# Four-layer graph network: the residual of the node stages formed per tile from PSUM, two small layer-norm operations on ScalarE

## What is computed

```
x = layernorm(x + L0(x, ...))      # out = self(x) * attr + conv * attr^2 ...
x = layernorm(x + L1(x, ...))
x = layernorm(x + L2(x, ...))
x = layernorm(x + L3(x, ...))      # cos(angle) * scfeat + sin(angle) * conv
layernorm(x) = (x - mean(x)) / sqrt(var(x) + 1e-5)
```

## Time and profile before

| | us |
|---|---|
| median of 3 runs | 4850.13 (4847.89 to 4857.97) |
| the profiled execution, its own time | 4907.07 |
| its span (first to last instruction) | 4905.3 |
| mean granted TensorE clock in it | 0.871 of full |
| busy in the span: PE / DVE / ACT / POOL | 3837.4 / 3538.7 / 2331.3 / 3500.2 |
| node stage of layer 0, first to last L1344 | 785.4 to 1222.0 |
| node stage of layer 1 | 2507.4 to 2761.6 |
| node stage of layer 2 | 3461.0 to 3741.7 |
| node stage of layer 3 | 4422.0 to 4897.8 |

### The profile page before, as it was taken

One profiled execution on the slowest core, in us unless ns is written; L12 is line 12 of the kernel. 1 busy time (PEld: TensorE's weight loads), 2 busy tenths in 40 slices (PEclk: granted clock), 3 DMA queues, 4 the chain that ended last, 5 costly groups with the idle time before them and its releaser, 6 DMA issues. The chain is left out here.

```text
span 4905.3 us, 72936 instructions
## 1 busy us (share of the span) xinstructions
PE 3837.4 (78%) x14102; PEld 1906.9 (39%) x14102; DVE 3538.7 (72%) x8505; ACT 2331.3 (48%) x6704; POOL 3500.2 (71%) x3640
## 2 busy tenths in 40 slices
PE   1999996776699999999920288888897888877666
PEld 0333334554244444444310133333674333335554
DVE  1666667999488888888868554544896555549999
ACT  0233323555455555555446543433896333335555
POOL 1666667999578877887634466666697666659998
PEclk9999997877799999999955598998998999988777
DMA  9222225665455555545469622222995222237665
GB/s 392 67 67 67 69 67 176 213 214 189 106 125 129 130 126 129 123 124 124 108 227 368 222 67 65 67 65 58 323 355 187 67 68 67 68 86 211 192 189 160
DMA packets 585571, 718.23 MB, mean 146 GB/s; under 512 B 79012, under 2 KB 409194, under 8 KB 585224
## 3 DMA queue, kind: packets, MB, share of 16 engines
q1 hardware_dynamic: 492812, 536.17, 36.1%
q0 software_dynamic: 86400, 142.71, 11.2%
q10 hardware_dynamic: 6268, 38.40, 1.9%
HBM read 488.77 MB, written 245.93 MB: 150 GB/s over the span
## 5 line engine op out<-in xcount | busy, mean ns | idle before, releaser
L539 POOL DMA_INDIRECT aggregates<-agg_out,scatter_index x600 | 615.8, 1026 | 400.9 <-issue 258.0
L1285 ACT ACTIVATE y_chunk<-residual,ln_minus_mean_rstd,ln_rstd 128x160 f32<-128x160 f32 x1568 | 691.7, 525 | 372.9 <-POOL ln_minus_mean_rstd L1348 287.9
L1344 POOL TENSOR_TENSOR ln_rstd<-ln_var_eps,minus_half 128x4 f32<-128x4 f32 x392 | 485.1, 1238 | 143.3 <-DVE ln_var_eps L1433 84.4
L1251 PE MATMUL psum<-self_weights,x_chunk_T 128*128 128x160 f32 (+1 forms) x2352 | 493.0, 362 | 64.7 <-DVE node_mid L1376 31.0
L522 POOL DMA_INDIRECT gathered<-x_layer,gather_index x400 | 395.5, 989 | 177.2 <-issue 118.6
L1251 PEld LDWEIGHTS psum<-self_weights,x_chunk_T 128*128 128x128 f32 x2352 | 414.1, 224 | 110.4 <-issue 63.2
L615 PE MATMUL psum<-identity,scaled_x 128*128 128x128 f32 x600 | 145.8, 282 | 373.6 <-DVE scaled_x L689 312.4
L1441 DVE BATCH_NORM_STATS2 ln_stats<-residual 128x6 f32<-128x160 f32 x1568 | 389.2, 307 | 0.1
L561 ACT ACTIVATE scaled_x<-gathered,sh_times_attr 128x160 f32<-128x160 f32 x400 | 138.4, 417 | 459.7 <-DVE sh_times_attr L672 307.0
L1329 POOL TENSOR_TENSOR agg_chunk<-agg_chunk,x_chunk 128x640 f32<-128x640 f32 x196 | 327.5, 1671 | 15.4
L638 PE MATMUL psum<-hidden,weights 64*128 64x512 f32 x300 | 185.8, 702 | 193.4 <-ACT hidden L573 131.4
(11 more groups left out here) (222 smaller groups left out, 10592.5 us busy)
## 6 DMA issues: line engine op xcount, KB each, us to landing
x_layer<-y_chunk SPq DMA_DIRECT2D x294, 320.0 KB, 5.3
x_chunk<-x_layer SPq DMA_DIRECT2D x294, 320.0 KB, 4.7
agg_chunk<-aggregates SPq DMA_DIRECT2D x196, 320.0 KB, 5.5
sh_rows<-in_sh_big SPq DMA_DIRECT2D x50, 768.0 KB
agg_chunk<-aggregates SPq DMA_DIRECT2D x98, 384.0 KB, 6.0
aggregates<-zero_rows ACTq DMA_DIRECT2D x1, 36864.0 KB
x_chunk<-in_x SPq DMA_DIRECT2D x98, 322.0 KB, 3.0
agg_chunk<-aggregates SPq DMA_DIRECT2D x98, 322.0 KB, 3.7
```

Source lines behind the costliest of these rows:

```text
L539: eng.indirect_dma_start(agg_table[:, :], bass.IndirectOffsetOnAxis(idx_last[:, q, b:b + 1], 0), agg_out[:, q, b, :], None, bounds_check=N ...
L1251: eng.matmul(o[:, b, 0:ns + 96], x_t[:, k4, (2 * half + b) * 128:(2 * half + b) * 128 + 128], self_w[:, k, 0:ns + 96], start=b == 0, stop= ...
L1285: op = eng.activation(y_out[:, buf, b, :], res[:, buf, b, :], ACT.Identity, bias=shift[:, buf, b:b + 1], scale=rstd[:, buf, b:b + 1])
L1344: eng.tensor_tensor(rstd[:, buf, :], var_eps[:, q, :], minus_half[:, 0:T], ALU.pow)\
```

## The change

In layers 0 and 3 the multiplication out of PSUM (L1376) and the addition (L1395) become one operation per tile, four per chunk, that reads PSUM, multiplies by a per-partition scalar and adds `agg_in`, and writes `res` directly. It stands where the multiplication stood in the step. It waits for what both waited for (`u_mm`, in layer 3 `half`, `agg_x`, and `applied` of four chunks before), and PE's wait for the PSUM buffer and POOL's for its buffer are now on `res`. In all four layers the two small operations on mean and variance leave DVE and stand on ACT, after L1285 and ahead of L1292, with the same waits. A constant column with epsilon is set up for them. Everything else stays.

```diff
@@ node_tensor
-                    wait(eng, S["mid"] if l == 2 else S["u_scaled"], c - 1)
+                    wait(eng, S["mid"] if l == 2 else S["res"], c - 1)
@@ node_scalar, after the four operations of L1285
+                lag = SUM[l] + 1
+                if live(s, lag, NC):
+                    c, buf, q = s - lag, (par - lag) % RB, (par - lag) % 2
+                    eng.wait_ge(S["aggr"], at(S["aggr"], c + 1))
+                    wait(eng, S["rstd"], c - 1)
+                    wait(eng, S["shift"], c - 1)
+                    eng.activation(var_eps[:, q, :].unsqueeze(2), mv[:, buf, :, 1:2], ACT.Identity, bias=eps_col[:, 0:1])\
+                       .then_inc(S["eps"], 1)
+                    eng.activation(neg_mean[:, q, :].unsqueeze(2), mv[:, buf, :, 0:1], ACT.Copy, scale=-1.0)\
+                       .then_inc(S["neg_mean"], 1)
@@ node_gpsimd
-                        wait(eng, S["u_scaled"], c - 1)
+                        wait(eng, S["res"], c - 1)
@@ node_vector, scaled_u
+                wait(eng, S["applied"], c - 3)
                 if l == 3:
                     eng.wait_ge(S["half"], at(S["half"], c + 1))
-                    by = turned[:, q, 0, :]
-                else:
-                    by = attr_all[:, bass.ds(c * T, T)]
-                eng.tensor_tensor(mid[:, q, :, 0:D], u[:, :, 0:D], by.unsqueeze(2).to_broadcast([128, T, D]), ALU.mult)\
-                   .then_inc(S["u_scaled"], 1)
+                eng.wait_ge(S["agg_x"], at(S["agg_x"], c + 1))
+                for b in range(T):
+                    by = turned[:, q, 0, b:b + 1] if l == 3 else attr_all[:, bass.ds(c * T + b, 1)]
+                    op = eng.scalar_tensor_tensor(out=res[:, r, b, :], in0=u[:, b, 0:D], scalar=by,
+                                                  in1=agg_in[:, buf, b, 0:D], op0=ALU.mult, op1=ALU.add)
+                op.then_inc(S["res"], 1)
@@ node_vector, residual
-                eng.wait_ge(S["u_scaled"], at(S["u_scaled"], c + 1))
-                eng.wait_ge(S["agg_x"], at(S["agg_x"], c + 1))
-                eng.tensor_tensor(res[:, r], mid[:, q, :, 0:D], agg_in[:, buf, :, 0:D], ALU.add).then_inc(S["res"], 1)
@@ node_vector, step: gone
-                    eng.tensor_scalar(var_eps[:, q, :].unsqueeze(2), mv[:, buf, :, 1:2], EPS, None, ALU.add)\
-                       .then_inc(S["eps"], 1)
-                    eng.tensor_scalar(neg_mean[:, q, :].unsqueeze(2), mv[:, buf, :, 0:1], -1.0, None, ALU.mult)\
-                       .then_inc(S["neg_mean"], 1)
```

More of the change, by code:

```diff
@@ L139, in gnn_kernel @@
         ones_col = sb("ones_column", [128, 1])
+        eps_col = sb("epsilon_column", [128, 1])
         ones_row = sb("ones_row", [1, GE])
@@ L258, in gnn_kernel @@
                                  "neg_mean res rstd shift stats store0 store1 store2 store3 tail transposed trig turn u_mm "
-                                 "u_scaled xt_copied")
+                                 "xt_copied")
         NODE = {l: node_sems for l in range(4)}
@@ L287, in node_counts @@
             if l not in (0, 3):
-                n.update(agg_scaled=0, agg_x=0, u_scaled=0)
+                n.update(agg_scaled=0, agg_x=0)
             n.update(turn=4 * NC, trig=NC, half=NC) if l == 3 else n.update(turn=0, trig=0, half=0)
@@ L318, in apart @@
         def apart(eng):
-            eng.wait_ge(P["consts"], 3)
+            eng.wait_ge(P["consts"], 4)
         def apart_from(eng, value):
@@ L391, in setup_gpsimd @@
             eng.memset(ones_col[:, :], 1.0).then_inc(P["consts"], 1)
+            eng.memset(eps_col[:, :], EPS).then_inc(P["consts"], 1)
             eng.memset(ident[:, :], 0.0).then_inc(P["ident0"], 1)
@@ L1263, in node_scalar @@
             S = NODE[l]
+            if l == 0:
+                eng.wait_ge(P["consts"], 4)
             def step(s, par):
@@ L1310, in step @@
                     held(eng, loaded(l, c, buf), S[f"load{buf}"])
-                    held(eng, c - 1, S["u_scaled"])
+                    held(eng, c - 1, S["res"])
                     held(eng, c * T)
@@ L1360, in node_vector, with scaled_u @@
             S = NODE[l]
-            def scaled_u(c, buf, q):
+            def scaled_u(c, buf, q, r):
                 u = psum[:, 4 + 2 * q:6 + 2 * q, :].rearrange("p a (b c) -> p (a b) c", c=256)
@@ L1405, in step @@
                 if l != 1 and live(s, U[l], NC):
-                    scaled_u(s - U[l], (par - U[l]) % NB, (par - U[l]) % 2)
+                    scaled_u(s - U[l], (par - U[l]) % NB, (par - U[l]) % 2, (par - U[l]) % RB)
                 if angles:
@@ L1422, in step @@
                        .then_inc(S["turn"], 1)
-                if live(s, SUM[l], NC):
+                if l in (1, 2) and live(s, SUM[l], NC):
                     residual(s - SUM[l], (par - SUM[l]) % NB, (par - SUM[l]) % RB, (par - SUM[l]) % 2)
```

## The result

Over 20 runs each the changed kernel takes 4831.42 us (4825.18 to 4845.28) and the kernel before 4859.06 (4847.89 to 4916.91); the ratio is 0.9934, 95% interval 0.9914 to 0.9954, so it is 22 to 42 us faster. I had forecast 60 us less, 4790; 4831.42 lies 1.4 us outside the range. The gain is real and about half of what was forecast.

The account below looks back on a forecast made before the run. The prediction took POOL to bound layers 0 and 3, DMA layer 1 and ACT layer 2. Layer 0 -43, layer 3 -46, layer 2 +28 and drains +1 gave -60 us, from 4850.13 to 4790 us, range 4762 to 4830.

Parts of the forecast that it names:

- What bounds each stage: Node stages: POOL bounds layers 0 and 3, DMA layer 1, ACT layer 2; DVE's 100% in layers 0 and 3 is blocking.
- Layer 0, -43: Layer 0: without L1395's blocking, POOL's L1329 takes 1.43 us instead of 1.879, over 95 steps: -43 us.
- part 2: All layers: epsilon and negated mean move from DVE to ACT; gains nothing in layers 0 and 3, costs 28 us in layer 2.
- Layer 3, -46: Layer 3: without the collision with L1395, POOL's power takes 1.01 us instead of 1.509, over 88 steps: -46 us.
- Layer 2, +28: Layer 2: ACT has no slack, so the two added small operations cost 0.29 us in each of 96 steps: +28 us.
- the remark that the two operations would be better off left on VectorE: The skill's rule keeps additions and multiplications on VectorE; with epsilon and negation left there, the sum would lack the +28.
- Layer 1, 0: Layer 1: ACT is busy 144 of 220 us, so DMA covers the added 0.29 us: no change.
- The new operation, 1.1 us for four: Layers 0 and 3, DVE: four per-tile operations take 1.1 us per chunk, ends 0.80 and 1.24; matters little.
- Rival (a): Layers 0 and 3: the new operations block POOL's power, 4985 us in full, 4844 in small; chance 0.05 each.
- The growth of the power: Sign of a wrong forecast: POOL's power (L1344) takes longer, where 1.02 us was expected in layer 3.
- Rival (b): Layers 0 and 3: PE at the low clock bounds the stages, steps of 5.1 us, total 4934 us; chance 0.03.
- The sum: Whole kernel: -43 - 46 + 28 + 1 = -60 us, taken from the runs' median of 4850.13 to 4790 us.

Follow-up runs that it names:

- experiments 7 and 8: Only the first layer (LAYERS = 1) of the kernel before (7) and of the changed kernel (8): 1234.34 and 1184.57 us.
- Experiment 3: Kernel before with only epsilon and negated mean moved from DVE to ACT, in all layers: 4845.18 us, ratio 0.9968.
- experiment 6: Kernel before with the new per-tile operation in layer 3 only: 4851.56 us, ratio 0.9998.
- experiment 4: Changed kernel with layer 2's epsilon and negated mean back on DVE: 4806.34 us, ratio 0.9885 to the kernel before.
- experiment 1: Kernel before, run again without edit: median 4861.18 us, ratio 1.0008; profiled 4921.91 us.
- experiment 9: Kernel before with two more small aggregations per chunk on DVE in layer 3, results unused: 4853.26 us, ratio 1.0002.
- experiment 12: Kernel before without its last layer (LAYERS = 3): 3745.32 us, beside 4864.15 for the whole kernel on the same chip.
- experiment 5: Kernel before with the new per-tile operation in layer 0 only: median 4801.39 us, ratio 0.9886; profiled 4853.84 us.

## Why the prediction was wrong

By its own steps:

- **What bounds each stage** was right: POOL in layers 0 and 3 (in layer 3 DVE still counts as 99% busy after, blocked time included), DMA in layer 1, ACT in layer 2. That DVE's 100% in layer 0 was blocking was right too; it is 59% now.
- **Layer 0, -43.** Measured -45.9 in the trace and -49.8 without the profiler (experiments 7 and 8). The size was right. Its cause was told too simply. I put it all on L1395 and wrote of part 2 that in layers 0 and 3 it "opens nothing". Experiment 3 shows that part 2 alone gives the 43 us of layer 0 as well, with L1395 in place. The two parts are two cures for one thing, a pattern in which the blocked small operation makes DVE late and late L1395 stretches POOL; their gains don't add.
- **Layer 3, -46.** This is the term that failed, by being booked for every execution. It measured -48.4 in the trace, and 0 in the runs (experiment 6: 0.9998). The mechanism within a step was read rightly, from the earlier trace rows side by side, but those rows showed both patterns in one stage, and with them that the stage can have either. The 88 steps of the earlier trace rows hold free steps as well (67 of the stage's 98 powers are stretched), so even the execution with the trace had both. What tips it, L1403 against L1326 by 0.02 us, had no place in the prediction.
- **Layer 2, +28**, measured +26.4, and 25 between the changed kernel and experiment 4. Right, and for layer 2 so was the remark that the two operations would be better off left on VectorE.
- **Layer 1, 0**, measured +0.7.
- **The new operation, 1.1 us for four**: 1.26 in layer 0, just above the upper end of 1.24. As forecast it mattered nothing; DVE waits 154 us in layer 0. From start to start one costs 0.29. Rival (a) is out: over all 784 of them it takes 364 to 386 ns, beside POOL or not, and the power beside it, in layers 0 and 3, is not stretched. The growth of the power, which the prediction named as a sign of being wrong, came in layers 1 and 2, from the other part, at no cost. Rival (b) is out: the granted clock is 0.97 in layer 0, and in layer 3, where it is 0.80, the step is 4.47 all the same.
- **The sum.** "I carry the difference over to the median unchanged": here it broke. The profiled execution was 57 us above the median of the runs and outside their range. That number was in the prediction and was passed over. 48 of it is layer 3's collision, and a gain from taking away what makes an execution slow can't be booked for the runs that don't have it. Without layer 3's term the sum is -43 + 28 + 1 = -14. With the sizes that the runs gave, -49.8 for layer 0 (experiments 7 and 8) and +25 for layer 2 (experiment 4), it is -25, against 28 measured (22 to 42), or 27 without the three long runs of before.

So the runs leave little open. In the traces the parts between the node stages differ as well, and no run separates why: layer 0's end to layer 1's start is 1285.5 us in before, 1290.5 in experiment 1, 1275.3 after. Layer 1's end to layer 2's start is 699 to 703 us in the five traces in which layer 0 collides (before, experiments 1, 6, 9 and 12), and 691 to 698 in the five in which it doesn't. Open too is why the profiled execution takes the long pattern so often. All three with layer 3's old code and order took it (before, experiments 1 and 5), against one of the 11 other runs of experiment 1, none of the 5 of experiment 5 and three of the 20 of the result. A race of 0.02 us at one place can be turned by little, but no execution without the profiler has a trace.

## What to carry to other kernels

Compare the profiled execution's own time with the runs first. When it lies outside their range, look for a stage whose step has two lengths in the trace, and book a gain that rests on the longer one only for the share of the runs that have it. Where two engines exclude each other, ask of an operation not only what it costs but what it makes late, for a blocked operation of 4 elements can keep a whole stage in its worse pattern. An operation moved to an engine that is saturated in one stage should stay where it was in that stage: the same change without layer 2's part (experiment 4) gained 56 us instead of 32, by the ratios.

## What the runs showed of the hardware

The exclusion between DVE and POOL is a matter of single operations. POOL's L1329 held back DVE's epsilon, an operation on 4 elements, so that it took 1.39 us instead of 0.15, in 92 of layer 0's 98 chunks. The power, though also on POOL and reading SBUF, held back nothing once it had started: the residual's addition in experiment 3 (L1409 there), with two SBUF tensors of 640 elements, started 0.17 us into it and took 0.83. If the power starts 0.02 us behind such an operation, it waits for it (1.67 us instead of 1.02, in 67 of layer 3's 98 chunks before). The other way round, a DVE operation that starts 0.02 to 0.04 us behind POOL's scaling gets through: L1403 took 0.14 to 0.15 us there (experiments 1 and 3), and 1.15 when it started 0.12 behind (experiment 9).

The Trainium skill (SBUF — State Buffer, Who interferes with whom) says that a DVE instruction with two SBUF inputs contends with a POOL instruction that reads SBUF, and of DVE's two-port modes that whoever issues first has the pair of ports that the two engines share for the whole instruction. The traces agree on the contention for POOL's 640-element operations. They differ for the power: it reads SBUF, and DVE's addition wasn't held once it had started, as if it let go early. The Trainium skill says in the same section that a DVE instruction with at most one SBUF input, outside the two-port modes, doesn't contend, and the new operation agrees, with one input in PSUM, one in SBUF and a scalar per partition from SBUF: in layer 3 of the changed kernel (timeline) four of them run into L1340 and take what they take alone, as does L1340:

```profile
4605.05 1.25 DVE L1391 SCALAR_TENSOR_TENSOR residual<-psum,cos_sin_times_attr,agg_chunk 128x160 f32<-128x160 f32 x4
...
4605.62 1.25 POOL L1340 TENSOR_TENSOR agg_chunk<-agg_chunk,cos_sin_times_attr 128x640 f32<-128x640 f32 x1
```
